# Two sets of filler matmuls taken out and three zone tiles moved from VectorE to ScalarE in a quantised FFN kernel

## The chip, the cores and the metric

The kernel runs on one core of one Trainium2 chip. The metric is the device time of one execution, in microseconds (us). TensorE (PE), VectorE (DVE), ScalarE (ACT) and GpSimd (POOL) compute; SyncE (SP) only issues DMAs here.

## What is computed

The reference, cut to what matters:

```python
# x: [64, 64, 512] float32; cond: 64 row numbers; weights: [200, 64, 64]; weight: [512, 512]; bias: [512]
y = jnp.einsum('bct,bcd->bdt', x, weights[cond])    # a 64x64 mix for each batch element
# _quant_dequant_mxfp4: in blocks of 32 along the last axis,
#   scale = 2 ** (floor(log2(amax)) - 2);  q = clip(y / scale, -6, 6)
#   lsb = 0.5, 1 or 2 by |q| < 2, < 4 or more;  result = round(q / lsb) * lsb * scale
a = _quant_dequant_mxfp4(y.reshape(-1, 512))
w = _quant_dequant_mxfp4(weight)
out = x + (jnp.einsum('mk,nk->mn', a, w) + bias)
```

## The kernel before

Two batch elements of 64 rows make one tile of 128x512; the 32 tiles are worked on in eight groups of four (`step` in the code, `LAST` = 8). The weights are quantised first, as group 0. `q` = 0 or 1 is the first or second pair of a group's tiles. A group goes through the engines like this:

- TensorE makes `y_ps` from `x_sb` and the gathered 64x64 matrices `mix` (`mix_pair(step, q)`, L360; called mix(step,q) in the text). It writes PSUM banks that the previous group's `y` must have left: it waits for `y_copied` (L357).
- ScalarE makes `z`, the magnitude in bfloat16, of each pair (`z_pair`, L539) and copies `y` to `y_sb` (`y_pair`, L547).
- VectorE finds the maximum of each block in a tree of three steps (`m`, L668, L674, L680) and a reduction (`amax`, L685); makes the scales `s` (`lowest_zone` L691, `top_zone` L698), lifts `z` to `low` (L703) and inverts it to `inv` (L708).
- `zone` is a linear function of the bits of `inv`. ScalarE makes it for tiles 0 and 1 (`zone_pair`, L555), VectorE for tiles 2 and 3 (`other_zones`, L721).
- VectorE rounds `y_sb` times `inv` to the integers `n_int` (`round_y`, L715, once for each pair), bounds the zones to `top` (`limit`, L734, which waits for both zones) and multiplies both to `a` (`rescale`, L743).
- TensorE turns `a` (`turn_pair`, L388) into `o_ps`, ScalarE copies it to `aT` (`copy_turned`, L581), TensorE adds x (`residual_pair`, L372), for tiles 0 and 1, and the bias by a matmul of three rows (`bias_tile`, L402), and multiplies with the turned weights (`ffn_tile`, L407).
- ScalarE copies tiles 0 and 1 out to `x_sb` (`copy_pair`, L560) and tiles 2 and 3 to `o_sb` (`copy_out`, L572), to which x is added by an accumulating DMA of GpSimd (L339). Groups 7 and 8 are finished by VectorE and by tile.

The order on each engine is written out by hand: every engine runs its own program, and semaphores join them. VectorE works on the quantisation of group `step` and on the block maxima of group `step` + 1 in turn. In its loop pass for a group, TensorE multiplies group `step` - 1, makes mix(step+2,1), adds x for the group, turns the group, adds the bias, and makes mix(step+3,0). ScalarE starts its pass with the zones, and goes on with `z`, `y`, the copies out, `z`, `y` and two `aT`.

`keep_busy(n)` (L432) issues n matmuls of a tile of zeros into a bank that is then unused; they compute nothing. They stand after each turning of the weights (32 and 56) and in group 1, 14 ahead of its turning and 20 behind it.

The bias rows come to `bias3` by six DMAs which GpSimd issues (L332) after the mixes of groups 2 to 4; TensorE's first bias matmul, in group 1, waits for all six (`bias3_in`, L478). x of each group is loaded by SyncE in order of need.

## Time and profile before

| | us |
|---|---|
| median of 3 runs | 93.13 |
| lowest and highest | 93.05, 93.2 |
| the profiled execution | 92.92 |
| its span, first to last instruction | 91.2 |
| TensorE busy | 83.4 (91%) |
| VectorE busy | 83.2 (91%) |
| ScalarE busy | 74.0 (81%) |
| GpSimd busy | 29.4 (32%) |

The granted TensorE clock is 1.000 over the span. Busy shares say little here, since two engines stand at 91% and fillers count as TensorE's work. What is to be read is the chain that ended last, which follows the last instruction back through whatever released each step, and the timelines of the engines side by side. In a timeline a row's start less the start of the row ahead is its pitch; neighbours overlap by about 0.1 us, so a row's duration is a little longer than what it costs in a series.

### The profile page before, as it was taken

How to read it: one execution, taken by the hardware profiler on the slowest of the kernel's cores; microseconds unless marked ns; L12 is line 12 of the kernel's file. 1: busy time of each engine (PE TensorE's matmuls, PEld its weight loads, DVE VectorE, ACT ScalarE, POOL GpSimd, SP SyncE). 2: the span in 40 equal slices, each digit the busy share in tenths (PEclk: the TensorE clock that was granted, in tenths of full speed). 3: DMA queues.
4: the chain of work that ended last, by engine and by line, in shares of the span. 5: the costliest groups of instructions: out<-in, count | busy, mean ns of one | idle time of the engine just before them, and what ended most of it. 6: DMA issues, size and time to landing. Idle time of an engine off the chain costs nothing.

```text
span 91.2 us, 2142 instructions
## 1 busy us (share of the span) xinstructions
PE 83.4 (91%) x707; PEld 40.7 (45%) x707; DVE 83.2 (91%) x149; ACT 74.0 (81%) x86; POOL 29.4 (32%) x55
## 2 busy tenths in 40 slices
PE   4999695996989999999999999999999999999950
PEld 4995164494482334333433253353324333534530
DVE  1189998999999999999999999999999999999970
ACT  3746179999798759999999999999999997796500
POOL 4377797799878914000400120030003000000000
PEclk9999999999999999999999999999999999999999
DMA  0998299999999999999899999999929947914595
GB/s 31 332 312 293 68 213 343 355 338 301 330 260 229 223 185 261 229 221 257 195 323 305 272 383 222 342 357 255 184 101 275 240 88 275 378 37 166 181 378 202
DMA packets 14635, 22.68 MB, mean 248 GB/s; under 512 B 4130, under 2 KB 4898, under 8 KB 14626
## 3 DMA queue, kind: packets, MB, share of 16 engines
q1 hardware_dynamic: 12096, 18.49, 67.1%
q0 software_dynamic: 1968, 3.16, 17.6%
q10 hardware_dynamic: 562, 0.92, 2.8%
q8 instruction: 5, 0.08, 0.4%
q14 instruction: 4, 0.03, 0.1%
HBM read 11.54 MB, written 8.39 MB: 218 GB/s over the span
## 4 chain that ended last, share of the span: by engine, by line
DVE 49%; PE 20%; issue 3%; DVEq 1%
DVE n_int L715 13%; DVE a L743 8%; DVE top L734 7%; DVE low L703 6%; PE o_ps L407 6%; PE y_ps L407 5%; DVE inv L708 3%; DVE zone L721 2%; PE o_ps L372 2%; DVE amax L685 2%; DVE m L674 2%; DVE m L680 1%; PE y_ps L388 1%; PE o_ps L397 1%; PE o_ps L388 1%
## 5 line engine op out<-in xcount | busy, mean ns | idle before, releaser
L407 PE MATMUL o_ps<-wT,aT 128*128 128x512 bf16 x104 | 24.9, 380 | 0.0
L715 DVE TENSOR_TENSOR n_int<-y_sb,inv 128x1024 int16<-128x1024 f32 (+1 forms) x18 | 19.6, 1099 | 0.3
L360 PE MATMUL y_ps<-x_sb,mix 64*64 64x512 f32 x128 | 17.0, 611 | 2.9 <-DMA x_sb<-in_x_dram 1.0
L539 ACT ACTIVATE z<-y_ps 128x1024 bf16<-128x1024 bf16 x16 | 16.3, 1035 | 4.0 <-PE y_ps L360 4.0
L216 POOL DMA_DIRECT2D mix<-in_L_cond_weights_dram x32 | 17.3, 542 | 5.4 <-issue 4.4
L435 PE MATMUL o_ps<-idle 128*128 128x128 bf16 x206 | 15.7, 239 | 1.2 <-DVE idle L753 1.2
L547 ACT COPY y_sb<-y_ps 128x1024 f32<-128x1024 f32 x16 | 16.3, 1039 | 0.0
L407 PEld LDWEIGHTS o_ps<-wT,aT 128*128 128x128 bf16 x104 | 9.1, 98 | 15.5 <-ACT aT L581 4.1
L435 PEld LDWEIGHTS o_ps<-idle 128*128 128x128 bf16 x206 | 13.7, 108 | 3.3 <-issue 2.9
L339 POOL DMA_DIRECT2D x_sb<-o_sb x5 | 4.5, 891 | 32.9 <-ACT o_sb L572 32.9
L555 ACT ACTIVATE zone<-inv 128x1024 int16<-128x1024 int16 (+1 forms) x13 | 11.9, 937 | 0.2 <-DVE inv L708 0.2
L734 DVE TENSOR_TENSOR top<-zone,s 128x2048 bf16<-128x2048 bf16 (+2 forms) x14 | 11.7, 835 | 0.3 <-ACT zone L555 0.3
L581 ACT COPY aT<-o_ps 128x1024 bf16<-128x1024 bf16 x12 | 11.8, 1036 | 0.1
L743 DVE TENSOR_TENSOR a<-n_int,top 128x2048 bf16<-128x2048 int16 (+2 forms) x14 | 11.8, 839 | 0.0
L703 DVE TENSOR_TENSOR low<-z,s 128x2048 bf16<-128x2048 bf16 (+1 forms) x10 | 11.1, 1114 | 0.1
L668 DVE TENSOR_TENSOR m<-z 128x1024 bf16<-128x1024 bf16 (+2 forms) x11 | 6.5, 588 | 3.1 <-ACT z L531 3.1
L388 PEld LDWEIGHTS o_ps<-ident,a 128*128 128x128 bf16 x112 | 6.3, 98 | 5.8 <-DVE a L743 4.2
L388 PE MATMUL o_ps<-ident,a 128*128 128x128 bf16 x112 | 7.6, 220 | 0.4 <-DVE a L743 0.4
L360 PEld LDWEIGHTS y_ps<-x_sb,mix 64*64 64x64 f32 x128 | 3.7, 131 | 8.8 <-issue 6.2
L372 PE MATMUL o_ps<-x_sb,ident_f 64*64 64x512 f32 x56 | 7.4, 600 | 0.0
L560 ACT COPY x_sb<-o_ps 128x1024 f32<-128x1024 f32 x6 | 6.4, 1064 | 0.0
L708 DVE TENSOR_SCALAR inv<-low 128x2048 int16<-128x2048 int16 (+1 forms) x10 | 6.4, 636 | 0.0
(59 smaller groups left out, 77.0 us busy)
## 6 DMA issues: line engine op xcount, KB each, us to landing
x_sb<-in_x_dram SPq DMA_DIRECT2D x4, 1024.0 KB, 9.5
out_dram<-x_sb SPq DMA_DIRECT2D x8, 512.0 KB, 3.7
out_dram<-x_sb SPq DMA_DIRECT2D x12, 256.0 KB, 5.8
x_sb<-in_x_dram SPq DMA_DIRECT2D x10, 256.0 KB, 7.0
x_sb<-o_sb POOLq DMA_DIRECT2D x5, 512.0 KB, 6.7
w_sb<-in_L_ffn_weight_dram SPq DMA_DIRECT2D x4, 256.0 KB, 3.2
x_sb<-in_x_dram SPq DMA_DIRECT2D x2, 512.0 KB, 8.0
last_x<-in_x_dram SPq DMA_DIRECT2D x1, 1024.0 KB, 6.1
```

The costliest lines, as they stand in the source:

```text
L216: queue.dma_start(mix[HALVES[half], tile, :], table[bass.ds(row, 1), :, :].rearrange("o c d -> (o c) d")).then_inc(done, 16)
L360: last = nc.tensor.matmul(y_ps[HALVES[g], 2 * q + r, :], mix[HALVES[r], (step - 1) * GROUP + n, :], x_tiles(step, n)[HALVES[r], :], start= ...
L388: last = nc.tensor.transpose(place, a2[:, 2 * q + r, c * P:(c + 1) * P], ident[:, :])
L407: last = nc.tensor.matmul(o_bank(step, t), aT[:, t, c, :], wT[:, c, :], start=False, stop=(c == KC - 1))
L435: nc.tensor.matmul(o_ps[:, 0, c * P:(c + 1) * P], idle[:, :], idle[:, :], start=True, stop=True)
L539: nc.scalar.activation(blocked(columns(z[:, step % 2, :, :], 2 * q, 2)), high_by_place(y_tiles(2 * q, 2)), ACT.Abs, scale=ZONE_GAIN).then_ ...
L547: nc.scalar.copy(blocked(columns(y_sb[:, step % 2, :, :], 2 * q, 2)), by_place(y_tiles(2 * q, 2))).then_inc(y_copied, 2)
L555: nc.scalar.activation(columns(zone, t0, n).bitcast(I16), columns(inv, t0, n).bitcast(I16), ACT.Copy, bias=float(EXPONENT - 2 * BINADE), s ...
L703: nc.vector.tensor_tensor(columns(low, t, n), columns(z[:, step % 2, :, :], t, n), spread(s1, t, n), ALU.max).then_inc(z_used, 1)
L715: nc.vector.tensor_tensor(columns(n_int, t, n), columns(y_sb[:, step % 2, :, :], t, n), columns(inv, t, n), ALU.mult).then_inc(n_done, 1)
L734: nc.vector.tensor_tensor(columns(top, t, n), columns(zone, t, n), spread(s3, t, n), ALU.min).then_inc(top_done, 1)
L743: nc.vector.tensor_tensor(a2[:, t:t + n, :].rearrange("p t (h k) -> p h t k", h=HI), columns(n_int, t, n).rearrange("p h (t k) -> p h t k" ...
```

## The change

In the loop pass of group 1, TensorE's fillers are taken out, 14 ahead of the turning and 20 behind it. After the second turning of the weights there are 64 fillers where there were 56. For groups 1, 2 and 7 (`ALL_ZONES`) ScalarE makes the zones of all four tiles, as two instructions in a row; the second counts up `other_zone_done`, which VectorE's instruction did. VectorE's order changes with it: in group 2 the block maximum goes behind `top` and the scale `s` behind `a`; in group 7 the first step of the tree goes between the two roundings.

```diff
+    ALL_ZONES = (1, 2, LAST - 1)
...
             turn_pair(0, 1, straight=True)
-            keep_busy(56)
+            keep_busy(64)
             mix_pair(3, 0)
...
                 mix_pair(step + 2, 1)
-                if step == 1:
-                    keep_busy(14)
-                elif step < LAST - 2:
+                if 1 < step < LAST - 2:
                     residual_pair(step, 0)
-                else:
+                elif step == LAST - 2:
...
                 if step == 1:
-                    keep_busy(20)
                     pe.wait_ge(ident_f_ready, 2)
                     residual_pair(step, 0)
...
-            def zone_pair(inverses, limits, t0=0, n=2):
+            def zone_pair(inverses, limits, t0=0, n=2, done=zone_done):
...
-                                     bias=float(EXPONENT - 2 * BINADE), scale=-1.0).then_inc(zone_done, 1)
+                                     bias=float(EXPONENT - 2 * BINADE), scale=-1.0).then_inc(done, 1)
+
+            def step_zones(step):
+                zone_pair(after(step), after(step - 1))
+                if step in ALL_ZONES:
+                    zone_pair(after(step), after(step - 1), 2, 2, done=other_zone_done)
...
-            zone_pair(after(1), after(0))
+            step_zones(1)
...
                 if step > 1:
-                    zone_pair(after(step), after(step - 1))
+                    step_zones(step)
...
-            zone_pair(after(LAST - 1), after(LAST - 2))
+            step_zones(LAST - 1)
...
                 if step == 1:
-                    other_zones(step)
                     tree_1(step + 1)
                     limit(step, after(step))
...
+                    lowest_zone(step + 3)
+                elif step in ALL_ZONES:
+                    tree_3(step + 4)
+                    limit(step, after(step))
+                    block_max(step + 3)
+                    rescale(step, after(step), 2 * step + 3)
                     lowest_zone(step + 3)
                 else:
...
             round_y(LAST - 1, 0)
+            tree_1(LAST)
             round_y(LAST - 1, 2)
-            tree_1(LAST)
-            other_zones(LAST - 1)
             tree_2(LAST + 3)
```

TensorE, from the second turning of the weights (`ident,a`) to the first bias of group 1, before:

```order
L388 MATMUL o_ps<-ident,a 128x128 x8
L435 MATMUL o_ps<-idle 128x128 x56
L360 MATMUL y_ps<-x_sb,mix 64x512 x8
L435 MATMUL o_ps<-idle 128x128 x14
L388 MATMUL o_ps<-ident,a 128x128 x8
L388 MATMUL o_ps<-ident,a 128x2x64 x8
L435 MATMUL o_ps<-idle 128x128 x20
L372 MATMUL o_ps<-x_sb,ident_f 64x512 x4
L402 MATMUL o_ps<-bias,ones 128x512 x2
L360 MATMUL y_ps<-x_sb,mix 64x512 x4
```

and after, where the line numbers of this function are two higher:

```order
L390 MATMUL o_ps<-ident,a 128x128 x8
L437 MATMUL o_ps<-idle 128x128 x64
L362 MATMUL y_ps<-x_sb,mix 64x512 x8
L390 MATMUL o_ps<-ident,a 128x128 x8
L390 MATMUL o_ps<-ident,a 128x2x64 x8
L374 MATMUL o_ps<-x_sb,ident_f 64x512 x4
L404 MATMUL o_ps<-bias,ones 128x512 x2
L362 MATMUL y_ps<-x_sb,mix 64x512 x4
```

Nothing stands between mix(3,1) and the turning of group 1, or between that and the adding of x. The eight new fillers stand ahead of mix(3,0).

ScalarE, from the last two copies of turned weights (`wT`) to the second `z` of group 4, before:

```order
L591 ACTIVATE wT<-o_ps 128x4x128 x2
L555 ACTIVATE zone<-inv 128x8x128
L547 COPY y_sb<-y_ps 128x8x128 x2
L539 ACTIVATE z<-y_ps 128x8x128 x2
L547 COPY y_sb<-y_ps 128x8x128
L581 COPY aT<-o_ps 128x1024 x2
L555 ACTIVATE zone<-inv 128x8x128
L539 ACTIVATE z<-y_ps 128x8x128
L547 COPY y_sb<-y_ps 128x8x128
L560 COPY x_sb<-o_ps 128x1024
L572 COPY o_sb<-o_ps 128x1024
L539 ACTIVATE z<-y_ps 128x8x128
```

and after:

```order
L595 ACTIVATE wT<-o_ps 128x4x128 x2
L554 ACTIVATE zone<-inv 128x8x128 x2
L546 COPY y_sb<-y_ps 128x8x128 x2
L538 ACTIVATE z<-y_ps 128x8x128 x2
L546 COPY y_sb<-y_ps 128x8x128
L585 COPY aT<-o_ps 128x1024 x2
L554 ACTIVATE zone<-inv 128x8x128 x2
L538 ACTIVATE z<-y_ps 128x8x128
L546 COPY y_sb<-y_ps 128x8x128
L564 COPY x_sb<-o_ps 128x1024
L576 COPY o_sb<-o_ps 128x1024
L538 ACTIVATE z<-y_ps 128x8x128
```

The second zone of groups 1 and 2 now stands ahead of the copies of `y`, of `z` and of the copies out.

VectorE in group 2, from the first rounding to `low` of group 3, before:

```order
L715 TENSOR_TENSOR n_int<-y_sb,inv 128x8x128
L674 TENSOR_TENSOR m<-m 128x512
L715 TENSOR_TENSOR n_int<-y_sb,inv 128x8x128
L680 TENSOR_TENSOR m<-m 128x256
L721 TENSOR_SCALAR zone<-inv 128x8x128
L685 TENSOR_REDUCE amax<-m 128x64
L734 TENSOR_TENSOR top<-zone,s 128x2048
L691 TENSOR_SCALAR s<-amax 128x256
L743 TENSOR_TENSOR a<-n_int,top 128x8x4x64
L703 TENSOR_TENSOR low<-z,s 128x2048
```

and after:

```order
L719 TENSOR_TENSOR n_int<-y_sb,inv 128x8x128
L678 TENSOR_TENSOR m<-m 128x512
L719 TENSOR_TENSOR n_int<-y_sb,inv 128x8x128
L684 TENSOR_TENSOR m<-m 128x256
L738 TENSOR_TENSOR top<-zone,s 128x2048
L689 TENSOR_REDUCE amax<-m 128x64
L747 TENSOR_TENSOR a<-n_int,top 128x8x4x64
L695 TENSOR_SCALAR s<-amax 128x256
L707 TENSOR_TENSOR low<-z,s 128x2048
```

`zone` is gone, `amax` is behind `top`, and `s` stands between `a` and `low`, which reads it.

## Rows read from the trace of the kernel before

**Rows 1.** Page, part 4: the chain that ended last, by engine.
```profile
DVE 49%; PE 20%; issue 3%; DVEq 1%
```

**Rows 2.** The chain in order of time: start us, us, what.
```profile
21.84 0.34 DVE zone L721
...
67.47 1.24 DVE a L743
...
68.75 1.07 PE o_ps L388 x16
```

**Rows 3.** Timeline of VectorE: start us, us, engine, line, operation, out<-in, form, xcount.
```profile
22.70 1.22 DVE L734 TENSOR_TENSOR top<-zone,s 128x2048 bf16<-128x2048 bf16 x1
...
26.07 0.29 DVE L691 TENSOR_SCALAR s<-amax 128x256 int16<-128x256 int16 x1
26.40 1.23 DVE L703 TENSOR_TENSOR low<-z,s 128x2048 bf16<-128x2048 bf16 x1
...
32.35 1.21 DVE L734 TENSOR_TENSOR top<-zone,s 128x2048 bf16<-128x2048 bf16 x1
33.48 0.28 DVE L691 TENSOR_SCALAR s<-amax 128x256 int16<-128x256 int16 x1
33.70 1.22 DVE L743 TENSOR_TENSOR a<-n_int,top 128x2048 bf16<-128x2048 int16 x1
```

**Rows 4.** Timeline of ScalarE, the same columns; in brackets idle time before, and its releaser.
```profile
20.08 1.13 ACT L555 ACTIVATE zone<-inv 128x1024 int16<-128x1024 int16 x1
21.03 2.01 ACT L547 COPY y_sb<-y_ps 128x1024 f32<-128x1024 f32 x2
23.52 1.94 ACT L539 ACTIVATE z<-y_ps 128x1024 bf16<-128x1024 bf16 x2 [0.48 <-PE y_ps L360]
...
28.39 1.06 ACT L555 ACTIVATE zone<-inv 128x1024 int16<-128x1024 int16 x1 [0.20 <-DVE inv L708]
30.16 1.02 ACT L539 ACTIVATE z<-y_ps 128x1024 bf16<-128x1024 bf16 x1 [0.70 <-PE y_ps L360]
...
34.06 1.01 ACT L572 COPY o_sb<-o_ps 128x1024 f32<-128x1024 f32 x1 [1.06 <-PE o_ps L407]
35.14 1.02 ACT L539 ACTIVATE z<-y_ps 128x1024 bf16<-128x1024 bf16 x1
...
75.93 1.01 ACT L572 COPY x_sb<-o_ps 128x1024 f32<-128x1024 f32 x1 [0.86 <-PE o_ps L407]
```

**Rows 5.** Timeline of TensorE's matmuls, the same columns.
```profile
18.22 3.29 PE L435 MATMUL o_ps<-idle 128*128 128x128 bf16 x56
22.27 2.00 PE L360 MATMUL y_ps<-x_sb,mix 64*64 64x512 f32 x16 [0.76 <-ACT y_sb L547]
...
25.44 1.07 PE L388 MATMUL o_ps<-ident,a 128*128 128x128 bf16 x16 [0.28 <-DVE a L743]
26.34 1.28 PE L435 MATMUL o_ps<-idle 128*128 128x128 bf16 x20
27.55 1.09 PE L372 MATMUL o_ps<-x_sb,ident_f 64*64 64x512 f32 x8
28.57 0.39 PE L402 MATMUL o_ps<-bias,ones 3*128 3x512 bf16 x2
...
33.90 1.09 PE L360 MATMUL y_ps<-x_sb,mix 64*64 64x512 f32 x8
...
67.17 1.09 PE L360 MATMUL y_ps<-x_sb,mix 64*64 64x512 f32 x8
68.20 0.39 PE L402 MATMUL o_ps<-bias,ones 3*128 3x512 bf16 x2
```

**Rows 6.** GpSimd's last issue of bias rows, and its time to landing.
```profile
L332 POOL DMA_DIRECT2D bias<-bias_b x1: 484/484/484, 21.4 to 21.4; - x1
...
DMA to landing us min/median/max: 6.7/6.7/6.7
```

**Rows 7.** Busy time by stretch: PE, PEld, DVE, ACT, POOL; then granted clock, DMA.
```profile
9.40:15.80 6.40, 4.53 (x57) 2.71 (x56) 6.00 (x14) 4.13 (x5) 5.19 (x10) 1.00 0.74 211
```

## The prediction, made before the changed kernel was run

> **What bounds the kernel now.** I read the chain that ended last first. VectorE holds 49% of the span and TensorE 20% [rows 1]. In order of time it is all VectorE from 21.84 to 68.70 us and all TensorE from 68.75 to the last additions; the hand-over is group 6's rescaled tile `a` at 67.47 and TensorE's turning of it at 68.75 [rows 2]. So a microsecond saved on VectorE before 68.7 counts, if TensorE, and ScalarE which feeds it, arrive at that turning earlier too. After it only TensorE's work counts.
>
> How close are they? TensorE's issue of mix(8,1) stands at 67.17, that of mix(4,1) at 33.90: 8.32 us for a group [rows 5]. VectorE's `a` goes from 33.70 [rows 3] to 67.47 [rows 2] in four groups: 8.44 each. VectorE's round is the longer one: in the middle groups `a` is ready before TensorE asks for it, by 0.12 us less in each group, and at group 6 TensorE waits for it for the first time: TensorE's bias ends at 68.59, 0.16 before the turning starts [rows 2, 5]. So with VectorE alone earlier the end comes only 0.16 earlier. The rest has to come from TensorE and ScalarE, and their start is set in groups 1 and 2.
>
> **VectorE, part by part.** The `zone` of tiles 2 and 3 costs 0.34 us of the chain [rows 2], in group 1 and again in group 2, where the pattern is the same. In group 2 two others change places. `s` stood between `top` and `a` at a pitch of 0.22 (33.48 to 33.70), hiding latency; now it stands straight ahead of `low`, as in group 1, where the pitch is 0.33 (26.07 to 26.40) [rows 3]. `a` is thus 0.22 earlier still, and `low` gives 0.33 back: 0.11 lost. Sum: 0.34 + 0.34 - 0.11 = 0.57 us for all that follows group 2. The ends: 0.68 if the swap costs nothing, 0.46 if it costs twice as much. I take 0.57, each pitch being that of the same shapes. In group 7 the missing `zone` frees another 0.34, and `tree_1` goes between the two roundings, at no cost of its own. But there VectorE is not on the chain: TensorE finds `a` ready while it has work of its own, and that is the cover. Counted at nothing; without the cover 0.34 would be gained.
>
> **ScalarE.** Each added zone costs it 0.95 us, the pitch from 20.08 to 21.03 [rows 4], and it ends 1.06 to 1.13 after its start. Group 1: zones at 20.08 and 21.03, the second done by 22.16. VectorE asks for it at 22.70 - 0.34 = 22.36 [rows 3]: 0.2 to spare. The copies of `y` that stood at 21.03 move to 21.98, so mix(3,0) goes from 22.27 to 23.22 [rows 5], which waits for the first of them, and the `z` pair from 23.52 to 24.47 [rows 4]. Five pieces at about 0.91 each follow (two `z`, one `y`, two `aT`), so ScalarE is free for group 2 at 29.02, not at 28.39 where it had waited for `inv`. Its two zones start at 29.02 and 29.97 and the second is done at 31.03. VectorE asked at 32.35 [rows 3]; two zones less and the block maximum (0.33, by the pitch of `s` to `low` beside it) now behind `top`, that is 31.34: 0.3 to spare. Then `z` at 30.92 (it was 30.16, after 0.70 idle), `y` at 31.83, `x_sb` at 32.72 and `o_sb` at 33.62. The last was at 34.06 after 1.06 idle for TensorE [rows 4]. So the 1.9 us of new work fit in the 0.20, 0.70 and 1.06 us that ScalarE idles here, if TensorE delivers early enough (the 0.48 ahead of 23.52 stays, since mix(3,0) moves with it). In group 7 the extra 0.95 fits mostly in the 0.86 idle before 75.93 [rows 4]; 0.09 is left over, and that copy has no one waiting in this stretch. Counted at nothing.
>
> **TensorE.** Taken out are 14 and 20 fillers. 20 took 1.28 us, 26.34 to the residual at 27.55 [rows 5], all on TensorE's own path; the 14 stood in a wait for `a` (turning at 25.44 after 0.28 idle). The 8 that are added end at 18.22 + 64 x 0.0588 = 21.98, before mix(3,0) can start at 23.22: hidden. Mix(3,1) follows the second copy of `y` (21.03 + 2.01 + 0.95 [rows 4]) at 24.12 and ends its issue, 1.02 for a pair (27.55 to 28.57 [rows 5]), at 25.14; `a` of group 1 is done at 25.10. So the turning starts at 25.14 for 25.44, the residual at 26.14 for 27.55, and TensorE reaches the bias at 27.16 for 28.57. Here a new wait appears. The bias rows come by six small DMAs of GpSimd; the last was issued at 21.4 and landed 6.7 us later, at 28.1 [rows 6]. Nothing ahead of it moves in GpSimd or the DMA queues. So of 1.41 us only 28.57 - 28.16 = 0.41 is left (0.06 for the wake, an estimate: `z` at 35.14 stands 0.15 behind the end of its mix, 33.90 + 1.09 [rows 4, 5]). Queued behind this wait are the bias, mix(4,0), the products of group 1 and mix(4,1). The last goes from 33.90 to 33.49, if its `y` copy is out: that ends at 32.84, 0.5 before. `z` behind it starts at 34.73 for 35.14 [rows 4], ScalarE being free from 34.56. The cycle of TensorE and ScalarE is thus 0.41 earlier and keeps its pitch of 8.32. At group 6 TensorE is ready at 68.59 - 0.41 = 68.18; for VectorE alone the turning could start at 68.75 - 0.57 = 68.18 as well. The two arrive together.
>
> **The sum.** The turning of group 6 goes from 68.75 to 68.18: 0.57 us. From there all of TensorE's work follows in one piece, with `aT`, `copy_late` and the stores led by it, so the end moves by as much. The profiled execution took 92.92 us (span 91.2); 92.92 - 0.57 = 92.35. The median of the runs, 93.13, stands 0.21 above it, so I forecast 93.13 - 0.57 = **92.56 us**. Ends of the terms: VectorE 0.46 to 0.68; TensorE 0.16 + 0.41, less what the bias lands later and more if it lands earlier. With the bias 0.2 late the gain is 0.37; with it early, VectorE's, up to 0.68. Own range 92.4 to 92.8.
>
> **Rivals.**
> (a) The cycle of TensorE and ScalarE does not start earlier, since the bias lands 0.3 to 0.5 later than here, or ScalarE holds it. For it: all four later groups take over whatever lag it has, and its margins at 28 to 35 us are tenths. Against it: bias and `y` both have known times. Gain 0.16 to 0.3: 92.85 to 92.97.
> (b) Nothing reaches the end. The change does what it says, but a wait in groups 3 to 7, hidden today behind the one for VectorE, eats the 0.57 us: 93.0 to 93.2. Against it, TensorE's pitch is the same four times over.
> (c) The third zone counts too, because TensorE waits for VectorE in group 7 by other waits than the trace names: 0.57 + 0.34 = 0.91, so 92.22.
> (d) Slower, by ScalarE. It pays 0.95 us for what costs VectorE 0.34, and VectorE's `top` waits for it twice. It decides once ScalarE's second zone of group 2, due at 31.03, is more than 0.3 late, and the kernel is slower once it is 0.3 + 0.57 late. If one zone's 0.95 isn't absorbed, TensorE's cycle starts 0.95 later against 0.16 of slack: 93.13 + 0.79 = 93.9. The idle in [rows 4] speaks against it.
> The Trainium skill (ScalarE: Activation LUTs, Rules for kernel authors) has it that adds and multiplies belong on VectorE, up to about 3 times faster in bf16. By that rule the change goes the wrong way; here the trace agrees on the ratio (0.95 to 0.34, or 2.8 [rows 2, 4]), but it is idle time of ScalarE that pays.
> (e) Slower, by TensorE's clock. The granted clock is 1.00, the level of 2.4 GHz, throughout, also in 9.40 to 15.80, where TensorE is busy 4.53 of 6.40 us [rows 7]. After the change it idles from 21.98 to 23.22 and from 27.16 to 28.16, so it is busy for 3.9 of 6.2 us, 64% where those rows have 71%: a little sparser than anything shown. If the clock fell to 1.2 GHz at 28, the 5.3 us of issue from the bias to mix(4,1) would take twice as long: up to 93.13 + 5 = 98, and 94 if it lasts a microsecond or so.
> The Trainium skill (TensorE: Matmul & The Clock Gate, Why this matters for your kernels) warns of idle gaps between bursts as what halves the clock. No gap of this trace did it, with the 0.76 us before 22.27 [rows 5] among them; the new one of 1.24 us has no row here.
>
> **How the numbers follow.** Forecast 0.60; (a) 0.12; (b) 0.08; (c) 0.08; (d) 0.05; (e) 0.07. Range 92.2 to 93.05: it holds the forecast, (a), (c) and most of (b), about 0.85, and is drawn for the shares, 93.05 being where nothing more than noise is left. A measurement of this kernel can tell about 0.2%, 0.19 us, from no change. Faster by more: forecast, (c) and over half of (a), 0.75. Within: 0.13. Slower: (d) and (e), 0.12.
>
> **What would show it.** In the profile after: `top` of groups 1 and 2 with no idle before it, and ScalarE's double zones near 20.1 and 29.0; group 1's residual straight behind the turning, then a TensorE wait of 0.9 to 1.0 us before the bias, ending near 28.2; mix(4,1) near 33.5; the turning of group 6 near 68.2; the span 90.6. A bias that starts later than 28.4, or a `z` of group 4 past 34.9, would mean (a). `top` waiting for ScalarE would mean (d), and a granted clock under 1.00, (e). What would make me wrong most simply is a wait of TensorE's in groups 3 to 6 that VectorE's lead covers today.

## The result, and the profile after

The changed kernel took 93.51 us (median of 20 runs, 93.09 to 95.22), the kernel before beside it 92.90 (20 runs, 92.44 to 93.68). The ratio is 1.0064, with a 95% interval of 1.0042 to 1.0086: slower by 0.6%, where 0.6% faster was forecast. Two of the changed kernel's executions, at 94.70 and 95.22 us, were in a slower state and stand outside the ratio. The profiled execution took 93.54 us with a span of 91.7; that of before had 91.2.

What makes this result instructive is that the three compute engines did nearly all that was predicted. Here is TensorE's timeline after, from group 1 on (start us, us, engine, line, operation, out<-in, form, xcount, and in brackets idle time before and its releaser):

```profile
18.03 3.74 PE L437 MATMUL o_ps<-idle 128*128 128x128 bf16 x64
23.01 2.00 PE L362 MATMUL y_ps<-x_sb,mix 64*64 64x512 f32 x16 [1.25 <-ACT y_sb L546]
24.95 1.07 PE L390 MATMUL o_ps<-ident,a 128*128 128x128 bf16 x16
25.95 1.09 PE L374 MATMUL o_ps<-x_sb,ident_f 64*64 64x512 f32 x8
27.80 0.39 PE L404 MATMUL o_ps<-bias,ones 3*128 3x512 bf16 x2 [0.76 <-DMA bias<-bias_b]
...
33.12 1.09 PE L362 MATMUL y_ps<-x_sb,mix 64*64 64x512 f32 x8
...
68.07 1.07 PE L390 MATMUL o_ps<-ident,a 128*128 128x128 bf16 x16 [0.24 <-DVE a L747]
...
75.00 0.61 PE L390 MATMUL y_ps<-ident,a 128*128 128x128 bf16 x8
```

The turning of group 1 follows mix(3,1) at once, x follows the turning, and TensorE then waits for the bias rows. Mix(4,1) is at 33.12 (33.90 before, [rows 5]) and the turning of group 6 at 68.07 (68.75, [rows 2]). ScalarE, same columns:

```profile
19.89 2.07 ACT L554 ACTIVATE zone<-inv 128x1024 int16<-128x1024 int16 x2
21.79 2.00 ACT L546 COPY y_sb<-y_ps 128x1024 f32<-128x1024 f32 x2
...
28.79 2.04 ACT L554 ACTIVATE zone<-inv 128x1024 int16<-128x1024 int16 x2
...
34.37 1.04 ACT L538 ACTIVATE z<-y_ps 128x1024 bf16<-128x1024 bf16 x1
```

And VectorE in groups 1 and 2, with no idle in brackets ahead of any row:

```profile
22.20 1.22 DVE L738 TENSOR_TENSOR top<-zone,s 128x2048 bf16<-128x2048 bf16 x1
...
31.27 1.22 DVE L738 TENSOR_TENSOR top<-zone,s 128x2048 bf16<-128x2048 bf16 x1
32.40 0.41 DVE L689 TENSOR_REDUCE amax<-m 128x64 bf16<-128x256 bf16 x1
32.73 1.21 DVE L747 TENSOR_TENSOR a<-n_int,top 128x2048 bf16<-128x2048 int16 x1
33.86 0.28 DVE L695 TENSOR_SCALAR s<-amax 128x256 int16<-128x256 int16 x1
34.18 1.23 DVE L707 TENSOR_TENSOR low<-z,s 128x2048 bf16<-128x2048 bf16 x1
```

The lead lasts to the last computation of the kernel, VectorE's final addition to `last_x`. Before:

```profile
88.08 0.41 DVE L855 TENSOR_TENSOR last_x<-o_ps,last_x 128x256 f32<-128x256 f32 x1
```

and after:

```profile
87.21 0.41 DVE L863 TENSOR_TENSOR last_x<-o_ps,last_x 128x256 f32<-128x256 f32 x1
```

It starts 0.87 us earlier, and the span is 0.4 to 0.5 longer. So 1.3 to 1.4 us were lost behind the last computation, where only stores are left. The waits of SyncE at the end show them (line, releaser: us in total, times, longest). Before:

```profile
SPq L296 <- DMA out_dram<-last_x: 1.6, 1, 1.6
```

and after:

```profile
SPq L298 <- DMA out_dram<-last_x: 3.0, 1, 3.0
```

1.6 has become 3.0, which is the whole of it. The last store, of the same 128 KB, lands 3.6 us after its issue where it took 2.3 (DMA issues of the last microseconds; before, then after):

```profile
out_dram<-last_x SPq DMA_DIRECT2D x1, 128.0 KB, 2.3
```

```profile
out_dram<-last_x SPq DMA_DIRECT2D x1, 128.0 KB, 3.6
```

The volume of data is the same. What differs is shown by the busy share of the 16 DMA engines in half-microsecond stretches (length, granted clock, DMA share, GB/s). Before:

```profile
89.50:90.00 0.50, 1.00 1.01 332
90.00:90.50 0.50, 1.00 0.56 186
90.50:91.00 0.50, 1.00 0.00 0
```

After:

```profile
88.50:89.00 0.50, 1.00 1.01 338
89.00:89.50 0.50, 1.00 0.75 252
89.50:90.00 0.50, 1.00 0.06 25
90.00:90.50 0.50, 0.98 0.06 23
90.50:91.00 0.50, 0.50 0.05 18
```

Before, all engines stop within 0.2 us of each other. After, they are nearly done at 89.5, earlier than before, and then a share of 0.06 stays busy for another 1.4 us. 0.06 is 1/16: one DMA engine has work left when fifteen have none. What gave it more work than the others? The list of queues has two entries of the kind "instruction", q8 and q14. The packets of q14 inside the span start between 20 and 42 us in both kernels, far from the end; q8 has one near it. In the window from 84 to 86 us before (queue: packets, MB, share of the 16 engines' time):

```profile
q8 instruction: 1, 0.02, 3.4%
```

and from 86 to 88 us after:

```profile
q8 instruction: 1, 0.02, 2.9%
```

Queue 8 brings instructions. It has five packets of 16 KB in either kernel, and each occupies one DMA engine for 0.9 to 1.6 us (2.9% of 16 engines over 2 us is 0.93). The last one starts at 84.5 us before and is over at 85.6, while the stores rest for most of that time. After, it starts at 86.3, half a microsecond into the burst of last stores, which lasts from 85.8 to 89.4. The granted clock of 0.50 in the last row above comes after TensorE's last matmul (87.1) and costs nothing.

The theory to be tested: the chip refills the engine's instructions as its program advances; with 26 fillers less in TensorE's program, which were 52 instructions (a weight load and a matmul each), TensorE reaches the point of its last refill later in the work, and the refill falls on the last stores. The rivals: the zones on ScalarE hold up something that the timelines above don't show, or the last stores delay each other, now that the additions behind them come earlier.

The packets of the trace, one by one, speak for the theory. While the refill of the changed kernel runs (86.34 to 87.27), 15.5 data packets are under way on average; from 87.3 to 89.3 it is 16.4 (neighbours on one engine overlap a little). Then, within 0.02 us of the refill's end, three data packets of 2 KB follow in a row that take 0.23, 0.23 and 0.20 us, where such a packet takes 0.08 to 0.09 in the median behind 86 us. The same three stand behind the last refill in 17 of the 18 traces of this document (in before_more26 nothing was stored near it), and in the changed kernel no other data packet behind 86 us takes over 0.12. In after_more39 they run alone, when the fifteen other engines have nothing left of that burst. So a refill costs its engine 0.93 us and about 0.40 more (0.66 less three times 0.085, the median), an estimate of 1.33 in all, against the 1.3 to 1.4 found above. The trace doesn't name the engine of a packet. That the three belong to the refill's engine, and that it is the one which ends last, is inferred from the times; why they are slow no run shows.

### The profile page after: what moved, and what is told of

Same layout as the page of the kernel before. It is cut to its first block, busy times and chain, and to the rows that moved or that the text cites. A ratio compares the mean times of both kernels' runs of the same rounds, so it can differ in the third digit from the quotient of the medians.

```text
span 91.7 us, 2085 instructions
## 1 busy us (share of the span) xinstructions
PE 80.6 (88%) x673; PEld 39.0 (43%) x681; DVE 82.4 (90%) x146; ACT 76.5 (83%) x89; POOL 29.1 (32%) x55
## 4 chain that ended last, share of the span: by engine, by line
DVE 48%; PE 20%; ACT 8%; issue 8%; SPq 6%; DMA 5%; DVEq 1%; ACTq 0%
DVE n_int L719 13%; DVE a L747 8%; PE o_ps L409 7%; DVE top L738 7%; DVE low L707 6%; DMA mix<-in_L_cond_weights_dram 5%; PE y_ps L409 4%; DVE inv L712 3%; ACT zone L554 3%; PE o_ps L374 2%; SPq L218 2%; ACT y_sb L546 2%; DVE m L678 2%; SPq L203 2%; DVE amax L689 2%
## 5 line engine op out<-in xcount | busy, mean ns | idle before, releaser
L409 PE MATMUL o_ps<-wT,aT 128*128 128x512 bf16 x98 | 23.5, 380 | 1.0 <-issue 1.0
L538 ACT ACTIVATE z<-y_ps 128x1024 bf16<-128x1024 bf16 x16 | 16.4, 1038 | 3.3 <-PE y_ps L362 3.3
L218 POOL DMA_DIRECT2D mix<-in_L_cond_weights_dram x32 | 16.7, 524 | 5.8 <-issue 4.7
L546 ACT COPY y_sb<-y_ps 128x1024 f32<-128x1024 f32 x16 | 16.4, 1041 | 0.0
L409 PEld LDWEIGHTS o_ps<-wT,aT 128*128 128x128 bf16 x104 | 9.1, 98 | 15.5 <-ACT aT L585 4.9
L437 PE MATMUL o_ps<-idle 128*128 128x128 bf16 x180 | 13.9, 239 | 1.2 <-DVE idle L757 1.2
L554 ACT ACTIVATE zone<-inv 128x1024 int16<-128x1024 int16 (+1 forms) x16 | 14.8, 972 | 0.0
L437 PEld LDWEIGHTS o_ps<-idle 128*128 128x128 bf16 x180 | 11.8, 107 | 2.8 <-issue 2.5
```

The source lines that it names most:

```text
L218: queue.dma_start(mix[HALVES[half], tile, :], table[bass.ds(row, 1), :, :].rearrange("o c d -> (o c) d")).then_inc(done, 16)
L409: last = nc.tensor.matmul(o_bank(step, t), aT[:, t, c, :], wT[:, c, :], start=False, stop=(c == KC - 1))
L437: nc.tensor.matmul(o_ps[:, 0, c * P:(c + 1) * P], idle[:, :], idle[:, :], start=True, stop=True)
L538: nc.scalar.activation(blocked(columns(z[:, step % 2, :, :], 2 * q, 2)), high_by_place(y_tiles(2 * q, 2)), ACT.Abs, scale=ZONE_GAIN).then_ ...
L546: nc.scalar.copy(blocked(columns(y_sb[:, step % 2, :, :], 2 * q, 2)), by_place(y_tiles(2 * q, 2))).then_inc(y_copied, 2)
L554: nc.scalar.activation(columns(zone, t0, n).bitcast(I16), columns(inv, t0, n).bitcast(I16), ACT.Copy, bias=float(EXPONENT - 2 * BINADE), s ...
```

## The experiments

Each kernel was timed in five rounds beside the kernel before on the same chip; a ratio is to that, with its 95% interval. "Tail" is SyncE's last wait for `last_x` in the profiled execution, 1.6 us before and 3.0 after. "Refill" is the start of q8's last packet.

### The two parts apart

**before_again** is the kernel before, unchanged.

> The kernel before, once more, for a second trace of its end. Theory T (the work of the engines ends earlier in the changed kernel, and its last stores land late for a reason that lies in the change): here the last VectorE addition ends 2.3 to 2.8 us before the end of the span, as in the first trace (88.49 of 91.2), and the last store lands 2.3 us after its issue. Rival R (the late landing in the one profile of the changed kernel is chance of that execution, and most of its executions lose their time elsewhere): the last landing scatters here as well, between 2.3 and 3.6 us. Ratio 1.000 within 0.2% for both.

Measured: 1.0006 [0.9978, 1.0033], 92.95 us against 92.83. Refill at 85.3, tail 2.0: between the two kernels in both. All of this execution was some 0.2 late (turning of group 6 at 68.92). Single executions differ by more than that from the start on: VectorE's `inv` of group 1 stands at 18.70 in after_more52 and at 19.18 in more52_again, which have the same text. So two traces can't be compared by their times alone, and below the engines' part is measured from that `inv` to the start of the last addition. Before:

```profile
18.69 0.69 DVE L708 TENSOR_SCALAR inv<-low 128x2048 int16<-128x2048 int16 x1
```

and after:

```profile
18.54 0.69 DVE L712 TENSOR_SCALAR inv<-low 128x2048 int16<-128x2048 int16 x1
```

That is 69.39 us before (69.47 in before_again) and 68.67 after.

**after_again** is the changed kernel.

> The changed kernel, once more, for a second trace. T: the turning of group 6 near 68.1 and the last addition near 87.6, as in the first trace, but the last store lands 3.6 us after its issue and the span is near 91.7; ratio 1.006. R: the last store lands in 2.3 us again, and the span is then 90.5 if nothing else is lost; or the engines' own schedule is later somewhere between 10 and 80 us, which the timelines will show.

Measured: 1.0054 [1.0031, 1.0078]; refill at 85.9, tail 2.5; `inv` to last addition 68.80. The loss repeats, and so does the engines' gain.

**fillers_only** is the kernel before with the edit of the fillers alone:

```diff
-            keep_busy(56)
+            keep_busy(64)
...
-                if step == 1:
-                    keep_busy(14)
-                elif step < LAST - 2:
+                if 1 < step < LAST - 2:
...
-                    keep_busy(20)
```

> The kernel before with the change of TensorE's fillers alone (14 and 20 out, 56 to 64). TensorE and ScalarE come 0.4 us earlier to groups 2 to 6, VectorE doesn't: the turning of group 6 stays near 68.7, the end gains 0 to 0.05 us. T says ratio 1.000 if it is the earlier end of the work that makes the stores late, and about 1.006 if the fillers' absence itself does. R: 1.000.

Measured: 1.0110 [1.0066, 1.0155]; refill at 86.3, tail 2.4. Neither expectation allowed for this much. The loss comes with the fillers. From `inv` to the last addition it is 69.40 us, as before: the engines neither gain nor lose by them. (The turning of group 6 is at 68.18 for 68.75, but `inv` is as much earlier, at 18.12 for 18.69.)

**zones_only** is the changed kernel with all fillers as before, that is, only the zones and VectorE's order are changed:

```diff
-            keep_busy(64)
+            keep_busy(56)
...
+                if step == 1:
+                    keep_busy(14)
...
+                    keep_busy(20)
```

> The changed kernel with TensorE's fillers put back as they were (56, 14 and 20). VectorE is 0.57 us earlier from group 2 on, but mix(3,0) goes from 22.3 to 23.2, and behind it the fillers, the residual and the bias go 0.6 later, so that mix(4,1) starts near 34.5 for 33.9. TensorE is then 0.45 later at the turning of group 6 (69.2) and the end of the work is 0.45 us later: ratio 1.005 by the walk along the engines. T adds a late landing to it if it comes with the zones (about 1.015); R adds nothing.

Measured: 1.0048 [1.0025, 1.0070], but the profiled execution was the fastest of its twelve (92.71 us; refill at 84.5, tail 1.6), so its trace need not show the whole loss. I had expected the 1.005 from a TensorE that comes later, mix(3,0) having to wait for ScalarE's second zone. The trace has such a delay, but a smaller one: 69.56 us from `inv` to the last addition for 69.39 to 69.47. More on it under zones_only_more26.

### The instruction refill moved

The start of TensorE's program has a hardware loop of four fillers, executed 21 times. The next kernels write more of these as plain instructions and execute the loop less often (17 rounds and 26 plain ones are 94 fillers for 84). That puts 26 (39, 52) matmuls more into the program's text, far from the end and ahead of all work, so that the refills come earlier in the work.

**after_more26**, **before_more26** and **fillers_only_more26** carry this edit on the three kernels:

```diff
-            with pe.Fori(0, WARMUPS) as _:
+            with pe.Fori(0, 17) as _:
                 keep_busy(KC)
+            keep_busy(26)
```

> The changed kernel, with 26 fillers written out behind the warm-up loop, whose rounds go from 21 to 17 (about the same time), so that TensorE's program is as long as that of the kernel before. Theory F: TensorE's instructions are fetched in blocks of 16 KB by one of the 16 DMA engines; taking out 26 fillers (52 instructions) moves the last fetch from 84.5 us, a lull of the stores, to 86 us, into the last burst of stores, and the stores of that one engine land 1.0 to 1.6 us late. F expects the last fetch near 83.6 here, the last store landed 2.3 us after its issue, the last addition near 87.6 and the span 90.3: the 0.57 us that the walk along the engines gives, ratio 0.994. Rival C (the missing fillers in group 1 cost by themselves, through TensorE's activity or clock, and the program's length doesn't matter): ratio 1.006 as for the changed kernel.

> The kernel before with the same 26 fillers behind a warm-up of 17 rounds. F: the last fetch moves from 84.5 to about 83, before the last burst by more than before; ratio 0.997 to 1.000, since in some executions of the kernel before the fetch reaches into the burst. C: 1.000.

> The kernel with the fillers' change alone (ratio 1.011), with 26 fillers behind a warm-up of 17 rounds. F: the last fetch is back near 84.5, ratio 0.999 to 1.001. C: 1.011, since the group 1 of TensorE is just as empty.

Measured: 0.9957 [0.9932, 0.9982] for the changed kernel, 0.9997 [0.9970, 1.0023] for the kernel before, 1.0021 [0.9992, 1.0049] for the fillers alone. Refills at 84.2, 80.4 and 84.3; tails 1.9, 1.5 and 1.6. One edit that computes nothing takes 1.0% off the changed kernel, 0.9% off the fillers alone, and nothing that can be measured off the kernel before, whose refill was already early enough. It isn't the engines that gain: from `inv` to the last addition it is 68.68, 69.41 and 69.40 us, as without the edit (68.67, 69.39 and 69.40). That answers the two rivals. In after_more26 the zones stand on ScalarE as in the changed kernel, and the last addition ends at 87.6 as there, so neither a hidden wait for the zones nor stores that crowd because the additions come earlier can be the cause of the loss.

**before_fewer26** goes the other way: it takes 26 matmuls out of the text of the kernel before, by a loop in the place of plain fillers. 46 fillers run there instead of 56, ahead of a wait for `y_sb`; all else is untouched.

```diff
-            keep_busy(56)
+            keep_busy(24)
+            with pe.Fori(0, 5) as _:
+                keep_busy(KC)
+            keep_busy(2)
```

> The kernel before, in which 30 of the 56 fillers behind the second turning of the weights come from a loop of 5 rounds of 4 (1.9 us for 1.2 us, hidden in TensorE's wait for y), so the program is 26 fillers shorter and the work of TensorE, its gaps and its timing in groups 1 to 8 are the same. F: the last fetch near 86, the last store late by 1 us or more, ratio 1.008 to 1.012. C: 1.000.

Measured: 1.0095 [1.0064, 1.0126]. Its five refills fall within 1 us of the changed kernel's, the last at 86.3, and the loss is there with no zone moved and with engines that keep their time (69.41 us from `inv` to the last addition for 69.39). This run is the plainest proof: the text is shorter, the work ends when it did, and the kernel is 0.9% slower. SyncE's last wait and the end of the DMA share (from 90 us), as in the changed kernel:

```profile
SPq L296 <- DMA out_dram<-last_x: 2.4, 1, 2.4
```

```profile
90.00:90.50 0.50, 1.00 0.07 25
90.50:91.00 0.50, 1.00 0.05 16
```

**after_end26** puts 26 fillers behind the last matmul of the changed kernel. Its program is as long as that of after_more26, but nothing ahead of the last work has moved.

```diff
             for half in range(2):
                 ffn_half(half)
+            pe.wait_ge(added, 5)
+            keep_busy(26)
```

> The changed kernel with the 26 fillers put behind TensorE's last matmul, where it waits for VectorE's additions of tiles 0 to 2 of group 8 and nobody waits for it. Theory F (the last fetch is set off by how far TensorE has come in its program, so only what stands ahead of that point moves it): the fetch stays near 86 us, ratio 1.004 to 1.008. Rival L (the length of the program as such cures it, wherever the instructions stand): ratio 0.996, as with the 26 ahead of everything.

Measured: 1.0065 [1.0034, 1.0096], as slow as the changed kernel; refill at 85.9 (1.11 us long), tail 2.7. So it is not the length of the program but where in it the work stands.

**after_more39** and **after_more52** push the refill further ahead: 39 and 52 matmuls in the text, with 15 and 13 rounds of the loop.

```diff
-            with pe.Fori(0, WARMUPS) as _:
+            with pe.Fori(0, 13) as _:
                 keep_busy(KC)
+            keep_busy(52)
```

> The changed kernel with 39 fillers behind a warm-up of 15 rounds. F: 13 fillers more than the 26 move the last fetch from 84.2 to about 82, where the stores are in a lull; ratio 0.994 to 0.996. If the remaining distance of the 26 from the walk's 0.57 us (0.40 measured) comes from fetches that still reach into the last burst in some executions, it is 0.994 here, else 0.996. L says nothing of a place: 0.996.

> The changed kernel with 52 fillers behind a warm-up of 13 rounds. F: the last fetch near 80, in the end of a burst of stores that no one waits for; ratio 0.994 to 0.996. If a fetch did harm wherever it fell among stores, it would be 1.00 or more.

Measured: 0.9954 [0.9926, 0.9981] and 0.9939 [0.9914, 0.9963], refills at 80.5, in a lull of the stores, and at 79.9, at the end of an earlier burst. The tail of after_more39, and of after_more52 alike, is the shortest of all:

```profile
SPq L298 <- DMA out_dram<-last_x: 1.5, 1, 1.5
```

Both are faster than the kernel before as well as the changed one (92.29 and 92.26 us against 92.86).

### What the zones are worth with the refill out of the way

**zones_only_more26** and **before_more26_again** carry the edit of after_more26 on zones_only and on the kernel before.

> The kernel with the zones' change alone, the fillers of group 1 in place, and 26 more behind a warm-up of 17 rounds, so that the last fetch goes from 84.5 to about 80. If the 1.0048 of the zones alone is the later TensorE of the walk (the walk's 0.45 us less the 0.20 of group 7), it is 1.002 to 1.005 again; if it was the fetch reaching into the last burst in most executions, 0.998.

> The kernel before with 26 fillers behind a warm-up of 17 rounds, once more. The last fetch near 80 us; ratio 0.998 to 1.000. Against more52_again it gives the worth of the change with the fetch early in both: the walk says 0.57 us, and with 0.20 for group 7 0.77 us, or 0.6 to 0.8%.

Measured: 0.9982 [0.9962, 1.0003], refill at 78.3, and 0.9974 [0.9946, 1.0002], refill at 80.4; tails 1.5. With an early refill, moving the zones without taking out the fillers is about as fast as the kernel before. The engines are not: from `inv` to the last addition it is 69.81 us in this trace and 69.56 in that of zones_only, for 69.39 to 69.47 before. So the zones alone make the work end 0.1 to 0.4 us later, at most 0.45%, which fits the later TensorE that I had expected, less the 0.20 of group 7 (next). The medians of this pair differ by 0.2 us the same way (92.84 and 92.63). Whether the rest of the 1.0048 was the refill stays open: the only trace of zones_only has the refill at 84.5 and the tail of 1.6 of the kernel before, and it is of its fastest execution.

**more26_zones_12** gives group 7's zone back to VectorE, in its old order:

```diff
-    ALL_ZONES = (1, 2, LAST - 1)
+    ALL_ZONES = (1, 2)
...
-            tree_1(LAST)
             round_y(LAST - 1, 2)
+            tree_1(LAST)
+            other_zones(LAST - 1)
```

> The changed kernel with 26 fillers behind a warm-up of 17 rounds (0.9957), and with group 7's zones and VectorE order as they were before, so that ALL_ZONES is groups 1 and 2. The prediction's step that group 7 brings nothing says 0.9957 again, within 0.2%. The rival, that TensorE waits for VectorE in group 7 too, says 0.34 us more: 0.9995.

Measured: 1.0011 [0.9984, 1.0038], where I had expected the 0.9957 of after_more26. The refill lay at 84.8, not 84.2, so with 26 matmuls more it was still near the edge, though the tail in the trace is 1.9 in both. The traces give 0.20 us of the difference (68.88 from `inv` to the last addition for 68.68); the other 0.3 us are not accounted for. The comparison was repeated with 52: **more52_zones_12** and **more52_again** (the same text as after_more52).

> The changed kernel with 52 fillers behind a warm-up of 13 rounds, and with group 7 as before (zones of all tiles on ScalarE in groups 1 and 2 alone). If group 7 brings what the traces show between the turnings of groups 6 and 7 (7.13 us with VectorE's zone, 6.93 without), the end is 0.20 us later than with group 7 changed: ratio 0.996 for 0.994. If the 0.5 us between 0.9957 and 1.0011 was all group 7's, 0.999. If it was fetch and scatter alone, 0.994.

> The changed kernel with 52 fillers behind a warm-up of 13 rounds, once more beside the others of this call. The last fetch near 80 us, the end 2.3 us behind the last addition; ratio 0.993 to 0.995.

Measured: 0.9941 [0.9911, 0.9972] (92.41 us) and 0.9907 [0.9877, 0.9937] (92.32 us, six runs; the two medians are only 0.09 us apart), refills at 79.4 and 80.5. The intervals overlap, so the times alone don't settle it. The timelines do: TensorE's turnings of groups 6 and 7 with VectorE's zone in group 7,

```profile
68.17 1.07 PE L390 MATMUL o_ps<-ident,a 128*128 128x128 bf16 x16 [0.22 <-DVE a L748]
...
75.30 0.61 PE L390 MATMUL y_ps<-ident,a 128*128 128x128 bf16 x8
```

and with ScalarE's,

```profile
68.67 1.07 PE L390 MATMUL o_ps<-ident,a 128*128 128x128 bf16 x16
...
75.60 0.61 PE L390 MATMUL y_ps<-ident,a 128*128 128x128 bf16 x8
```

7.13 us from the one to the other against 6.93. The same numbers stand in the other traces: 7.13 in the kernel before (68.75 to 75.88), 6.93 in the changed one (68.07 to 75.00), and 6.91 to 6.93 or 7.13 in all others, by where the third zone is. The one exception is before_more26_again with 6.91, whose TensorE came late to group 6 and found `a` waiting. From the turning of group 7 to the last addition it is 12.20 to 12.22 us in all 18 traces. So the third zone is worth 0.20 us at the end of the work, as long as TensorE is not late itself.

### All runs side by side

Sorted by how long before the end of VectorE's last addition the refill starts:

| kernel | refill starts | addition ends | lead | tail | ratio |
|---|---|---|---|---|---|
| after | 86.3 | 87.6 | 1.3 | 3.0 | 1.0064 |
| fillers_only | 86.3 | 87.9 | 1.6 | 2.4 | 1.0110 |
| after_again | 85.9 | 87.6 | 1.7 | 2.5 | 1.0054 |
| after_end26 | 85.9 | 87.6 | 1.7 | 2.7 | 1.0065 |
| before_fewer26 | 86.3 | 88.2 | 1.9 | 2.4 | 1.0095 |
| before_again | 85.3 | 88.7 | 3.4 | 2.0 | 1.0006 |
| after_more26 | 84.2 | 87.6 | 3.4 | 1.9 | 0.9957 |
| more26_zones_12 | 84.8 | 88.2 | 3.4 | 1.9 | 1.0011 |
| zones_only | 84.5 | 88.2 | 3.7 | 1.6 | 1.0048 |
| fillers_only_more26 | 84.3 | 88.2 | 3.9 | 1.6 | 1.0021 |
| before | 84.5 | 88.5 | 4.0 | 1.6 | 1 |
| after_more39 | 80.5 | 87.6 | 7.1 | 1.5 | 0.9954 |
| more52_again | 80.5 | 88.2 | 7.7 | 1.5 | 0.9907 |
| after_more52 | 79.9 | 87.8 | 7.9 | 1.5 | 0.9939 |
| before_more26 | 80.4 | 88.4 | 8.0 | 1.5 | 0.9997 |
| more52_zones_12 | 79.4 | 87.9 | 8.5 | 1.5 | 0.9941 |
| before_more26_again | 80.4 | 89.2 | 8.8 | 1.5 | 0.9974 |
| zones_only_more26 | 78.3 | 88.8 | 10.5 | 1.5 | 0.9982 |

With a lead of over 7 us the tail is 1.5 every time, at 3.4 to 4.0 it is 1.6 to 2.0, and below 2 it is 2.4 to 3.0, whatever was done to the zones. It is the lead that counts and not a lull: the refills of before_more26_again and zones_only_more26 fell into a burst of stores, with 15 engines busy beside them, and the tail is 1.5. A ratio covers six to twenty executions of the kernel, the other columns one, which may be why zones_only doesn't fit its ratio.

The engines' part, from `inv` of group 1 to the start of the last addition:

| kernels | us |
|---|---|
| zones as before (before, before_again, before_more26, before_fewer26, fillers_only, fillers_only_more26) | 69.39 to 69.47 |
| zones moved, fillers as before (zones_only, zones_only_more26) | 69.56, 69.81 |
| the change without group 7 (more26_zones_12, more52_zones_12) | 68.88, 68.89 |
| the whole change (after, after_again, after_end26, after_more26, after_more39, after_more52, more52_again) | 68.63 to 69.03, mean 68.77 |

Left out is before_more26_again (70.50), in which x came late and the clock fell (last section). By this measure the change makes the work end 0.65 us earlier in the mean, in the kernels that come out slower (68.67, 68.80 and 69.03) as in those that come out faster.

## Why the prediction was wrong, step by step

- **VectorE, 0.57 us.** Right. From `inv` of group 1 to `low` of group 3 it is 16.15 us before (18.69 to 34.84) and 15.64 after (18.54 to 34.18), 0.51 less; five of the six other traces of the changed text have 15.58 to 15.64, so the worth is 0.51 to 0.57. `low` of group 3 is 0.66 earlier in all, the rest being an execution that started 0.15 earlier.
- **ScalarE's double zones.** Right: 19.89 and 28.79 for 20.08 and 29.02 predicted, early like all else; `z` of group 4 at 34.37, behind mix(4,1) as it was. `top` waited for neither, so rival (d) is out for this execution. The 0.2 us to spare were real, and all of them: in after_end26, where VectorE was further ahead, `top` of group 1 comes 3.86 us behind `inv` and not 3.66, right behind ScalarE's second zone (19.93 + 2.02 = 21.95 for 22.04). The ratio of 2.8 between the engines stands, and the idle time of ScalarE paid for it.
- **The new wait for the bias.** Right in kind and place: 0.76 us idle, the bias at 27.80 for 28.16 predicted; the DMA landed earlier, with the rest. The turning of group 6 is at 68.07 for 68.18, with both engines there within 0.24. Rival (a) is out for this execution but not in general. In after_again, after_end26 and after_more39 TensorE waited 1.03 to 1.12 us for the bias, the turning of group 6 follows the bias by 40.03 or 40.04 us with no wait for VectorE, and from `inv` to that turning only 0.16 to 0.39 us are gained for 0.51 to 0.57 in the other four. That is the mechanism of (a) with about its price, in three traces of seven; "With the bias 0.2 late the gain is 0.37" was well put.
- **Rival (b), a wait in groups 3 to 7 that eats the gain.** Out: the gain is there at the last addition in all seven traces of the changed text.
- **Group 7, counted at nothing.** Mis-sized: it is worth 0.20 us. Rival (c) had the place and 0.34. The working read that TensorE has work of its own whenever `a` is ready there. It had for part of the time only.
- **TensorE's clock, rival (e).** Out. The new stretch is 4.43 us of work in 6.20, 71%, with gaps of 1.25 and 0.76, and the granted clock stays at 1.00, the 2.4 GHz level:

```profile
22.00:28.20 6.20, 4.43 (x46) 1.78 (x50) 6.10 (x11) 5.72 (x7) 5.12 (x11) 1.00 1.08 275
```

- **"From there all of TensorE's work follows in one piece, with `aT`, `copy_late` and the stores led by it, so the end moves by as much."** This step failed. It holds up to the last addition, which starts 0.87 us earlier: 0.15 by the earlier start, 0.53 by the turning of group 6 and 0.20 in group 7 (rounded). It does not hold for the stores. They are led by VectorE's additions, but they share the 16 DMA engines with the refill of TensorE's instructions, and the change moved that from 84.5 to 86.3. Price: 0.9 to 1.5 us of tail in the profiled executions with a lead below 2 us (2.4 to 3.0 for 1.5). In the ratios, 1.0 to 1.3% (1.0064, 1.0054 and 1.0065 with a late refill, 0.9954 and 0.9939 with an early one), about 1 us. 0.7 us gained and 1.4 lost are the 0.6% by which the kernel is slower.

With the refill early on both sides (0.9954, 0.9939 and 0.9907 against 0.9997 and 0.9974) the change is worth 0.5% by the mean ratios, 0.9933 against 0.9985, and 0.4% by the medians of the same runs: 0.4 to 0.5 us, where the traces have 0.65. The forecast's 0.57 lies between them, but that is in part luck: it lacked the 0.20 of group 7, and it counted on a bias that is early enough, which it isn't always. Neither part brings the gain alone: 1.0021 for the fillers, 0.9982 for the zones, and in the traces nothing and 0.1 to 0.4 us lost. That agrees with the reading that VectorE and the pair of TensorE and ScalarE were within 0.16 us of each other at group 6, so that both had to come earlier.

Two small slips in the working change nothing: 93.13 - 0.30 is 92.83 and not 92.85 in (a), and 21.03 + 2.01 + 0.95 is 23.99, so that mix(3,1) at 24.12 holds 0.13 us that no row is named for.

In the costing of the fillers, each was priced by its time on TensorE alone, and "Nothing ahead of it moves in GpSimd or the DMA queues" was said of the bias rows alone; no sentence asks what moves behind them. The page of before lists q8 with five packets, but nothing in the prediction asked when they come, what they share, or what decides when. The Trainium skill (Runtime: NRT & Kernel Launch, Instruction fetch mechanics) says that an engine's instructions are refilled in blocks of 16 KiB or 256 instructions by a DMA queue of its own, and that the crossing of such a block is mostly hidden. The trace agrees on the size (five packets, 0.08 MB), and no row here shows TensorE waiting for one; the runs differ on hidden, since the block can hold up stores of data.

What stays open: that q8 carries TensorE's instructions is inferred. Its last packet moves with what is taken out of or put into TensorE's text ahead of the end, in zones_only, which has TensorE's text as before, it stands at 84.5 as before, and of the five engines only TensorE has instructions in the number (1,354 matmuls and weight loads in the profile after; VectorE 146). Why the three data packets behind a refill are slow was not found. And a typical execution of zones_only was not traced.

## What to carry to other kernels

The length and position of an engine's instruction text is a cost outside that engine: look at when the instruction queue's last packet comes against the last burst of stores, before and after any edit that adds or removes many instructions. If a change makes the engines earlier and the kernel later, compare the last computation's end with the span's end first; a DMA share of 1/16 in the tail says that one DMA engine alone has work left. Useless instructions at the program's head (26 to 52 matmuls here), in place of rounds of a loop, moved the refill 2 to 6 us further ahead of the last computation and took about 1 us off the changed kernel. And compare the engines from a point behind the start (here `inv` of group 1): between two executions of one text that point moved by 0.48 us (18.70 and 19.18), nearly as much as the change was to bring.

## What the runs showed of the hardware that was not expected

- A refill of instructions is one packet of 16 KB on one of the 16 DMA engines, 0.88 to 1.75 us long in these traces and 0.93 in the changed kernel's last burst. Three data packets of 0.23, 0.23 and 0.20 us follow the last one, where the median is 0.08 to 0.09. In the last burst of stores it makes SyncE's last wait 0.9 to 1.5 us longer (2.4 to 3.0 against 1.5).
- Its time follows the instructions' position: 26 matmuls less in the text moved the last refill from 84.5 to 86.3 us (before_fewer26, and the change itself), 26 more from 84.5 to 80.4 (before_more26), while 26 behind the end moved nothing that mattered (85.9 in after_end26 and in after_again). The same text scatters too: the last refill stands at 84.5 and 85.3 in the kernel before, and the second at 36.8 and 42.2 in the changed one.
- The granted clock can fall in this kernel, though not by this change. One execution of before_more26_again had x late, and TensorE waited 2.35 us ahead of its mixes of group 2. In the stretches behind it the granted clock (the number after the five engines) was down to 0.50, the 1.2 GHz level, and came back:

```profile
16.00:18.00 2.00, 1.52 (x12) 0.63 (x16) 1.90 (x4) 0.70 (x2) 1.50 (x3) 0.77 1.02 376
18.00:20.00 2.00, 2.00 (x13) 0.46 (x6) 1.90 (x4) 1.28 (x2) 1.93 (x4) 0.50 1.09 324
20.00:22.00 2.00, 2.00 (x34) 2.00 (x32) 2.00 (x4) 2.00 (x4) 2.00 (x6) 0.87 1.08 346
22.00:24.00 2.00, 2.00 (x36) 1.80 (x36) 1.62 (x3) 2.00 (x3) 1.89 (x4) 1.00 1.07 291
```

That execution took 93.46 us against a median of 92.63 of the same kernel, and its turning of group 6 was at 69.63, 1.04 later than in before_more26.
